# A DLRM tower with three interaction layers on one core: two steps of 32 rows in front, the top network in five chunks, and layer 1's sums on ScalarE

## Chip, core and metric

The kernel runs on one core of a Trainium2 chip. The metric is device time in microseconds (us), here the median of three executions. Five engines matter: TensorE (PE; its weight loads are shown as PEld), VectorE (DVE), ScalarE (ACT), GpSimd (POOL), and SyncE (SP), whose queue issues nearly all transfers. Each engine takes its own instructions in order; semaphores order the engines among themselves.

## What is computed

For 1024 batch rows, 32 table rows of 16 numbers are looked up (one of each table), which gives `e` with shape (1024, 32, 16). Three layers of pairwise products follow, each summed over the last dimension; the 192 sums and 16 dense numbers go through a small network.

```python
x0 = xk = e                                    # (1024, 32, 16)
for W in (W0, W1, W2):                         # (32, 32, 64), (32, 64, 64), (32, 64, 64)
    xk = relu(einsum('bmd,bhd,mhk->bkd', x0, xk, W))
    outs.append(sum(xk, axis=2))
z = concatenate(outs, axis=1)                  # (1024, 192)
h = concatenate([z, dense_ctx], axis=1)        # (1024, 208)
h = maximum(h @ W_top1 + b_top1, 0)            # 512
h = maximum(h @ W_top2 + b_top2, 0)            # 256
y = h @ W_top3                                 # (1024, 1)
```

All numbers are float32.

## The kernel before

**Steps.** The batch is cut into 16 steps of 64 rows. With 16 numbers a row, a step has 1024 columns (`PAIR`), handled as two halves of 512. Both halves of a layer's result lie in one PSUM bank: half 0 in partitions 0 to 63, half 1 in 64 to 127.

**Tiles.** For layers 1 and 2 the 32 x 64 = 2048 pairs (m, h) make 16 tiles of 128 partitions. A tile of x0, shifted by so many fields, is multiplied element by element with x1 or x2, and PE contracts the product with that tile's 64-column weights into the bank, one matmul for each half (`contract`). The trace shows each float32 matmul as two records, so a tile is four records. Layer 0 uses symmetry: one matmul pair over the squares and four tiles.

**Who multiplies.** DVE makes the products of layer 0 (two groups of two tiles) and of most tiles of layers 1 and 2, two tiles in one instruction (`product`), into a ring of four groups (`RING`, `prod`). POOL makes the last 3 tiles of layers 1 and 2 (5 and 4 in the last two steps, `POOL_LAST`), into a ring of four tiles. `POOL_BEFORE` says ahead of which DVE group PE takes each of POOL's tiles.

**Data in.** POOL gathers the rows of step s+2 with 16 indirect DMAs, spread between its tiles of step s: after the three tiles of layer 1 come 1, 1 and 8 gathers, after those of layer 2 come 1, 1 and 4. For the first two steps it issues all 32 gathers at the start. SP stores the gathered rows of a step to a scratch tensor in memory (`store_rows`), waits for that, loads the step's `x0g` (one transfer) and its 16 shifted tiles `x0bc` (`load_tiles`). `x0bc` has 24 slots of one tile, so tile j of step s waits until the product of 24 tiles earlier is made. SP does all this in program order.

**ACT.** For each layer, `finish` reads the bank: four ACTIVATEs spread relu(result) into x1_ps or x2_ps for DVE (`spread_done`), one writes `relu` in SBUF, four copy that to x1_sb or x2_sb for POOL (`copied`). Layer 2 has none of those; its 32 sums a step are made by 32 ACTIVATEs of 16 columns with an accumulator output, each followed by a read of the accumulator (L373). The sums of layers 0 and 1 are made by DVE, one TENSOR_REDUCE each (`sums`, L314). ACT also copies x0g into PSUM for DVE's layer 0 (`place_x0g`, L353) and squares it (L358).

**Order.** DVE runs layer 1 of step s, layer 0 of step s+1, sums of layer 0, layer 2 of step s, sums of layer 1. PE uses the same order over two banks that alternate (`STAGES`, `y_bank`), and waits for ACT to be done with a bank. ACT's order within a step:

```python
for s in range(STEPS):
    if s < LAST:
        place_x0g(s + 1)
        square(s + 1)
    finish(s, 1, x2_ps, x2_sb)
    if s < LAST:
        finish(s + 1, 0, x1_ps, x1_sb)
    else:
        mlp(range(MLP_EARLY))
    finish(s, 2)
mlp(range(MLP_EARLY, len(MLP)))
```

**Top network.** It works on two chunks of 512 rows. Its weights are loaded into free `x0bc` slots near the end. The first layer of chunk 0 (`MLP_EARLY`, 16 matmul records on PE) runs between layers 1 and 2 of the last step; everything else comes behind the last layer 2, and the 1024 results leave in one transfer.

Of the kernel before, what the change touches and what calls it, by code (L numbers as in the profile page):

```python
# [6 lines left out]
I32 = mybir.dt.int32  # L7
# [18 lines left out]
STEPS = COLS // PAIR  # L26
STEP_B = BATCH // STEPS
HALF_B = STEP_B // 2
QUART = P // FIELDS
GATHERS = STEP_B // QUART  # L30
# [15 lines left out]
POOL_LAST = {STEPS - 2: (5, 4), STEPS - 1: (5, 4)}  # L46
POOL_COUNT = [POOL_LAST.get(s, (3, 3)) for s in range(STEPS)]
POOL_BEFORE = {3: [2, 3, 5], 4: [2, 3, 4, 5], 5: [2, 3, 4, 5, 5]}
GATHERS_AFTER = {1: [1, 1, 8], 2: [1, 1, 4]}

# [29 lines left out]
def pool_after(x):  # L80
# [3 lines left out]
MLP = ([(1, 0, j) for j in range(HID1 // P)] + [(2, 0, j) for j in range(HID2 // P)] +  # L84
       [(1, 1, j) for j in range(HID1 // P)] + [(3, 0, 0)] + [(2, 1, j) for j in range(HID2 // P)] + [(3, 1, 0)])
MLP_EARLY = HID1 // P
MLP_BANKS = 4
LAST = STEPS - 1

# [5 lines left out]
def cin_tower_kernel(nc, table, ids, id_offset, dense_t, w0_a, w0_b, w0_sq, w1, w2,  # L95
                     wt1_a, wt1_b, bt1, wt2, bt2, wt3, x0_rows, out):
    with ExitStack() as ctx:
# [9 lines left out]
        ids_sb = sb("ids_sb", [P, STEPS * GATHERS], I32)  # L107
        off_sb = sb("off_sb", [P, STEPS * GATHERS], I32)
        row_sb = sb("row_sb", [P, STEPS * GATHERS], I32)
# [13 lines left out]
        z = sb("z", [P, 3, STEPS * HALF_B])  # L123
# [25 lines left out]
        mlp_ps = [x0g_ps[:, 0, :], x0g_ps[:, 1, :], x1_ps[:, 0, :], x1_ps[:, 1, :]]  # L149
# [387 lines left out]
```

## Time and profile before

| what | before |
|---|---|
| median of 3 runs | 637.69 us (637.17 to 637.77) |
| the profiled execution's own time | 638.89 us |
| span of its trace | 637.1 us |
| PE busy | 563.1 us (88%) |
| DVE busy | 548.7 us (86%) |
| POOL busy | 488.3 us (77%) |
| ACT busy | 302.5 us (47%) |
| transfers on SP's queue | 148.4 MB, 63.6% of 16 engines |

Busy shares are averages over stages with different limits: a front of about 60 us, a steady part, and a tail of about 50 us behind the last layer 1. Matmul records overlap, so a busy PE isn't PE at its peak. In what follows, (s, l) is layer l of step s, and "layer 0 of step s+1" is run by all engines behind (s, 1).

### The profile page before, as it was taken

How to read it: one execution, taken by the hardware profiler on the slowest of the kernel's cores; microseconds unless marked ns; L12 is line 12 of the kernel's file. 1: busy time of each engine (PE TensorE's matmuls, PEld its weight loads, DVE VectorE, ACT ScalarE, POOL GpSimd, SP SyncE). 2: the span in 40 equal slices, each digit the busy share in tenths (PEclk: the TensorE clock that was granted, in tenths of full speed). 3: DMA queues.
4: the chain of work that ended last, by engine and by line, in shares of the span. 5: the costliest groups of instructions: out<-in, count | busy, mean ns of one | idle time of the engine just before them, and what ended most of it. 6: DMA issues, size and time to landing. Idle time of an engine off the chain costs nothing.

```text
span 637.1 us, 7625 instructions
## 1 busy us (share of the span) xinstructions
PE 563.1 (88%) x2440; PEld 178.9 (28%) x2440; DVE 548.7 (86%) x330; ACT 302.5 (47%) x1359; POOL 488.3 (77%) x364
## 2 busy tenths in 40 slices
PE   0058998999999998999899999999999989999998
PEld 0012232332323232332223232323232322333332
DVE  0038998999999999999999999999999999897810
ACT  0023637354545646364535456464736454544352
POOL 6756898869888888979898788888897989584500
PEclk9997999999999999999999999999999999999999
DMA  3298857677876867686778768686868587871000
GB/s 105 39 391 312 307 200 284 240 298 263 306 274 227 295 217 270 244 299 214 297 274 306 268 238 315 211 298 215 307 213 319 225 302 266 307 284 49 1 1 0
DMA packets 52843, 151.01 MB, mean 237 GB/s; under 512 B 9697, under 2 KB 17377, under 8 KB 52802
## 3 DMA queue, kind: packets, MB, share of 16 engines
q1 hardware_dynamic: 44610, 148.40, 63.6%
q0 software_dynamic: 8192, 2.11, 2.5%
q8 instruction: 19, 0.31, 0.2%
q14 instruction: 22, 0.18, 0.1%
HBM read 147.33 MB, written 3.15 MB: 236 GB/s over the span
## 4 chain that ended last, share of the span: by engine, by line
DVE 36%; PE 24%; DMA 19%; issue 10%; POOL 8%; SPq 2%; ACT 1%; DVEq 0%; POOLq 0%
DVE prod L286 34%; PE y_ps L417 20%; DMA x0bc<-x_rows 15%; POOL emb L247 6%; DVE z L314 2%; DMA emb<-table,row_sb 2%; DMA x_rows<-emb 2%; POOL pool_prod L260 1%; SPq L214 1%; PE x_ps L477 1%; ACT relu L373 1%; PE x0g_ps L477 1%; PE x_ps L470 1%; PE x0g_ps L470 1%; PE x0g_ps L471 1%
## 5 line engine op out<-in xcount | busy, mean ns | idle before, releaser
L286 DVE TENSOR_TENSOR prod<-x0bc,x_ps 128x2048 f32<-128x2048 f32 (+1 forms) x252 | 456.0, 1878 | 8.6 <-ACT x_ps L368 8.6
L417 PE MATMUL y_ps<-prod,w_sb 128*64 128x512 f32 x1640 | 384.9, 599 | 27.8 <-DVE prod L286 27.8
L247 POOL DMA_INDIRECT emb<-table,row_sb x256 | 244.9, 957 | 65.5 <-issue 63.7
L260 POOL TENSOR_TENSOR pool_prod<-x0bc,x_sb 128x1024 f32<-128x1024 f32 x102 | 242.3, 2382 | 45.7 <-ACT x_sb L383 36.3
L417 PEld LDWEIGHTS y_ps<-prod,w_sb 128*64 128x64 f32 x1640 | 115.5, 137 | 280.1 <-issue 219.7
L373 ACT ACTIVATE relu<-y_ps 128x16 f32<-128x16 f32 x512 | 84.5, 287 | 144.3 <-PE y_ps L417 144.3
L368 ACT ACTIVATE x_ps<-y_ps 64x512 f32<-64x512 f32 x128 | 73.0, 570 | 78.5 <-PE y_ps L417 75.8
L417 PE MATMUL y_ps<-pool_prod,w_sb 128*64 128x512 f32 x408 | 105.0, 595 | 1.5 <-POOL pool_prod L260 1.3
L286 DVE TENSOR_TENSOR prod<-x0bc,x0g_ps 128x2048 f32<-128x2048 f32 x32 | 72.6, 2282 | 38.5 <-DMA x0bc<-x_rows 35.3
L373 ACT ACTIVATION_READ_ACCUMULATOR relu<-y_ps 128x1 f32 x512 | 84.7, 315 | 0.2
L383 ACT ACTIVATE x_sb<-relu 64x512 f32<-64x512 f32 x128 | 80.4, 628 | 3.4
L417 PE MATMUL y_ps<-prod,w0s_sb 128*64 128x512 f32 x256 | 61.6, 617 | 5.4 <-DVE prod L286 5.4
L353 ACT ACTIVATE x0g_ps<-x0g 128x1024 f32<-128x1024 f32 x16 | 16.4, 1028 | 90.1 <-DMA x0g<-x_rows 90.1
L417 PE MATMUL y_ps<-squares,wsq_sb 128*64 128x512 f32 x64 | 17.4, 623 | 35.6 <-ACT squares L358 35.6
L417 PEld LDWEIGHTS y_ps<-pool_prod,w_sb 128*64 128x64 f32 x408 | 28.3, 137 | 62.7 <-issue 47.8
L417 PEld LDWEIGHTS y_ps<-prod,w0s_sb 128*64 128x64 f32 x256 | 18.1, 141 | 47.1 <-issue 29.3
L314 DVE TENSOR_REDUCE z<-relu 128x32 f32<-128x512 f32 x32 | 21.6, 676 | 0.0
L378 ACT ACTIVATE relu<-y_ps 128x512 f32<-128x512 f32 x32 | 19.1, 597 | 0.8
L417 PEld LDWEIGHTS y_ps<-squares,wsq_sb 128*64 128x64 f32 x64 | 4.6, 141 | 44.1 <-issue 44.1
L358 ACT ACTIVATE squares<-x0g 128x1024 f32<-128x1024 f32 x16 | 16.7, 1041 | 0.0
L327 DVE COPY x0bc<-z 64x256 f32<-64x256 f32 x12 | 3.4, 286 | 11.6 <-ACT relu L373 11.3
L477 PE MATMUL x0g_ps<-x0bc 128*128 128x512 f32 x24 | 10.7, 597 | 0.0
(29 smaller groups left out, 49.2 us busy)
## 6 DMA issues: line engine op xcount, KB each, us to landing
x0bc<-x_rows SPq DMA_DIRECT2D x256, 512.0 KB, 6.8
x0g<-x_rows SPq DMA_DIRECT2D x16, 512.0 KB, 4.7
emb<-table,row_sb POOLq DMA_INDIRECT x256
x_rows<-emb SPq DMA_DIRECT2D x16, 128.0 KB, 2.1
w_sb<-w SPq DMA_DIRECT2D x2, 512.0 KB, 4.6
x_rows<-emb SPq DMA_DIRECT2D x16, 64.0 KB, 2.0
x0bc<-wt SPq DMA_DIRECT2D x1, 512.0 KB, 5.4
x0bc<-wt_a SPq DMA_DIRECT2D x1, 256.0 KB, 4.1
```

What stands on the lines that cost most here:

```text
L247: pool.indirect_dma_start(emb[:, turn, DIM * n:DIM * (n + 1)], None, table, bass.IndirectOffsetOnAxis(row_sb[:, at:at + 1], 0)).then_inc(g ...
L260: pool.tensor_tensor(pool_prod[:, n % POOL_RING, :], x0bc[:, slot(s, j), :], x[:], ALU.mult).then_inc(pool_products, 1)
L286: made = dve.tensor_tensor(prod[:, n % RING, 0:count, cols], tiles[:, :, cols], right.unsqueeze(1).to_broadcast([P, count, right.shape[1]] ...
L314: dve.tensor_reduce(z[:, l, s * HALF_B:(s + 1) * HALF_B], relu[:, l, :].rearrange("p (b d) -> p b d", d=DIM), AX_X, ALU.add).then_inc(summ ...
L353: act.activation(x0g_ps[:].rearrange("p h c -> p (h c)"), x0g[:], ACT.Copy).then_inc(x0g_placed, 1)
L358: act.activation(squares[:], x0g[:], ACT.Square).then_inc(squared, 1)
L368: act.activation(x[MAPS * copy:MAPS * (copy + 1), h, :], ps[MAPS * h:MAPS * (h + 1), :], ACT.Relu).then_inc(spread_done[l], 1)
L373: act.activation(relu[:, l, DIM * b:DIM * (b + 1)], ps[:, DIM * b:DIM * (b + 1)], ACT.Relu, accum_out=z[:, l, s * HALF_B + b:s * HALF_B + ...
L378: act.activation(relu[:, l, :], ps[:], ACT.Relu).then_inc(relu_done[l], 1)
L383: act.activation(x_sb[MAPS * copy:MAPS * (copy + 1), HALF * h:HALF * (h + 1)], relu[MAPS * h:MAPS * (h + 1), l, :], ACT.Copy).then_inc(cop ...
L417: made = pe.matmul(ps[MAPS * h:MAPS * (h + 1), :], w, moving[:, HALF * h:HALF * (h + 1)], start=first, stop=final)
L477: made = pe.matmul(ps[0:rows, :], w[:, k, :], x[:, k, :], start=k == 0, stop=k == ks - 1)
```

## The change

Four things are done at once.

1. The steps become 17: two of 32 rows, then 15 of 64. All widths become functions of the step. POOL has no tiles in step 0 and three half-wide tiles a layer in step 1. At the start POOL issues 8 + 8 + 16 gathers, for three steps. `off_sb` is one column, broadcast.
2. The top network runs in five chunks (steps 0 to 4, 5 to 8, 9 to 12, 13 to 15, and 16; 256, 256, 256, 192 and 64 rows). A chunk that ends ahead of step s (`TURN`: s = 5, 9, 13, 16) has its first layer on PE behind layer 0 of step s+1, its second behind (s, 2), and its third inside (s+1, 1) ahead of group 1. For s = 16 the second and third stand inside (16, 2), ahead of groups 2 and 4. They use x0g_ps as their bank. ACT makes the transposed input (`mlp_input`, 6 small copies, 12 for chunk 0), all relus, the copy of y, and issues the output transfer of each chunk. All weights have buffers of their own and are loaded by SP behind the tiles of step 1.
3. The sums of layer 1 move from DVE to ACT: 32 accumulating copies a step (`sums1`), read from `relu` in SBUF.
4. The sums of layer 2 in the last step alone go to DVE as one TENSOR_REDUCE; the last chunk's first layer adds its layer-2 part last (`last_chunk`).

The core of the diff:

```diff
-STEPS = COLS // PAIR
+ROWS_OF = [32, 32] + [64] * 15
+STEPS = len(ROWS_OF)
...
-POOL_LAST = {STEPS - 2: (5, 4), STEPS - 1: (5, 4)}
+POOL_OF = {0: (0, 0), STEPS - 2: (5, 4), STEPS - 1: (5, 4)}
...
+CHUNKS = [(0, 5), (5, 9), (9, 13), (13, 16), (16, 17)]
+FINAL = len(CHUNKS) - 1
+TURN = {end: c for c, (_, end) in enumerate(CHUNKS[:FINAL])}
...
 # SP
                 load_x0g(s)
                 load_tiles(s)
+                if s == 1:
+                    for dst, src in ((wt1a_sb[:], wt1_a), (wt1b_sb[:], wt1_b), (wt2_sb[:], wt2), (wt3_sb[:], wt3),
+                                     (bt1_sb[:], bt1), (bt2_sb[:], bt2), (zt_b[MAPS:, :], dense_t)):
+                        sp.dma_start(dst, src).then_inc(mlp_in, 16)
...
 # POOL
-            gather(0, 0, GATHERS)
+            gather(0, 0, GATHERS_OF[0])
             pool.wait_ge(rows_done, 2)
-            gather(1, 0, GATHERS)
+            gather(1, 0, GATHERS_OF[1])
+            gather(2, 0, GATHERS_OF[2])
...
 # DVE
                 sums(s, 0)
-                if s == LAST:
-                    mlp_input(0)
                 layer(s, 2, x2_ps)
-                sums(s, 1)
-            mlp_input(1)
+            sums(LAST, 2)
+            last_input()
...
 # ACT
+            def sums1(s):
+
+                for b in range(ROWS_OF[s] // 2):
+                    cols, at = slice(DIM * b, DIM * (b + 1)), FIRST_ROW[s] // 2 + b
+                    act.activation(spare[:, cols], relu[:, 1, cols], ACT.Copy,
+                                   accum_out=z[:, 1, at:at + 1]).then_inc(act_summed1, 1)
...
             for s in range(STEPS):
+                if s - 1 in TURN:
+                    hidden2(TURN[s - 1])
+                    output(TURN[s - 1])
+                if s in TURN:
+                    mlp_input(TURN[s], range(3))
                 if s < LAST:
                     place_x0g(s + 1)
                     square(s + 1)
                 finish(s, 1, x2_ps, x2_sb)
                 if s < LAST:
                     finish(s + 1, 0, x1_ps, x1_sb)
-                else:
-                    mlp(range(MLP_EARLY))
+                sums1(s)
+                if s in TURN:
+                    hidden1(TURN[s])
+                if s == LAST:
+                    hidden2(TURN[s])
+                    output(TURN[s])
+                    mlp_input(FINAL, range(2))
                 finish(s, 2)
-            mlp(range(MLP_EARLY, len(MLP)))
+            hidden1(FINAL)
+            hidden2(FINAL)
+            output(FINAL)
...
 # PE
+            def hidden2(c):
+                n = CHUNK_ROWS[c]
+                pe.wait_ge(mlp_act, PIECES_OF_CHUNK * c + H1_TILES)
+                for j in range(H2_TILES):
+                    for k in range(H1_TILES):
+                        made = pe.matmul(x0g_ps[:, 0, CHUNK_B * j:][:, 0:n], wt2_sb[:, k, P * j:P * (j + 1)],
+                                         h1[:, k, 0:n], start=k == 0, stop=k == H1_TILES - 1)
+                made.then_inc(mlp_mm, 1)
+
+            def output(c):
+                n = CHUNK_ROWS[c]
+                pe.wait_ge(mlp_act, PIECES_OF_CHUNK * c + H1_TILES + H2_TILES)
...
             for s in range(STEPS):
-                layer(s, 1, w1_sb)
+                layer(s, 1, w1_sb, {1: lambda: output(TURN[s - 1])} if s - 1 in TURN else {})
                 if s < LAST:
                     layer0(s + 1)
+                if s in TURN:
+                    pe.wait_ge(mlp_in, 16 * 7)
+                    hidden1(TURN[s])
+                if s == LAST:
+                    layer(s, 2, w2_sb, {2: lambda: hidden2(TURN[s]), 4: lambda: output(TURN[s])})
                 else:
-                    pe.wait_ge(mlp_in, 16 * 7)
-                    mlp(range(MLP_EARLY))
-                layer(s, 2, w2_sb)
-            mlp(range(MLP_EARLY, len(MLP)))
+                    layer(s, 2, w2_sb)
+                    if s in TURN:
+                        hidden2(TURN[s])
+            last_chunk()
```

## Rows read from the trace of the kernel before

**Rows 1.** Stages: length, busy of PE, PEld, DVE, ACT, POOL, clock, DMA share, GB/s.

```profile
36.50:61.00 24.50, 18.83 (x60) 5.02 (x58) 19.01 (x10) 6.34 (x10) 14.16 (x12) 0.86 0.93 342
102.00:554.00 452.00, 425.15 (x1918) 133.68 (x1916) 445.24 (x259) 235.86 (x1090) 382.95 (x282) 1.00 0.74 266
608.50:637.10 28.60, 24.95 (x58) 9.36 (x56) 1.73 (x6) 11.93 (x74) 0.00 (x0) 1.00 0.00 0
```

**Rows 2.** Waits from 102 to 554 us: total, times, longest.

```profile
ACT relu L373 <- PE y_ps L417: 114.7, 13, 9.8
...
ACT x0g_ps L353 <- DMA x0g<-x_rows: 45.6, 13, 4.3
...
POOL pool_prod L260 <- ACT x_sb L383: 14.2, 13, 2.6
...
DVE prod L286 <- DMA x0bc<-x_rows: 5.5, 7, 1.9
```

**Rows 3.** Groups by line and form: busy us, mean ns | idle before them.

```profile
L373 ACT ACTIVATION_READ_ACCUMULATOR relu<-y_ps 128x1 f32 x512 | 84.7, 315 | 0.2
L373 ACT ACTIVATE relu<-y_ps 128x16 f32<-128x16 f32 x512 | 84.5, 287 | 144.3 <-PE y_ps L417 144.3
L383 ACT ACTIVATE x_sb<-relu 64x512 f32<-64x512 f32 x128 | 80.4, 628 | 3.4
...
L378 ACT ACTIVATE relu<-y_ps 128x512 f32<-128x512 f32 x32 | 19.1, 597 | 0.8
...
L353 ACT ACTIVATE x0g_ps<-x0g 128x1024 f32<-128x1024 f32 x16 | 16.4, 1028 | 90.1 <-DMA x0g<-x_rows 90.1
```

**Rows 4.** The chain that ended last, 343 to 385 us: start, us, what.

```profile
344.28 1.89 DVE prod L286
...
348.76 0.60 DVE z L314
...
365.85 2.34 DMA emb<-table,row_sb
...
372.09 6.01 DMA x0bc<-x_rows
...
378.63 2.11 DVE prod L286
```

**Rows 5.** POOL's timeline in the same stretch: start, us, instruction.

```profile
352.45 2.37 POOL L260 TENSOR_TENSOR pool_prod<-x0bc,x_sb 128x1024 f32<-128x1024 f32 x1 [2.06 <-ACT x_sb L383]
...
366.80 2.38 POOL L260 TENSOR_TENSOR pool_prod<-x0bc,x_sb 128x1024 f32<-128x1024 f32 x1
```

**Rows 6.** Timeline of all engines, 0 to 60 us.

```profile
13.37 0.94 POOL L247 DMA_INDIRECT emb<-table,row_sb  x1 [0.30 <-issue]
...
23.35 0.94 POOL L247 DMA_INDIRECT emb<-table,row_sb  x1 [0.30 <-issue]
...
29.33 10.80 SPq L214 DMA_DIRECT2D x0bc<-x_rows  x16
...
36.46 4.71 DVE L286 TENSOR_TENSOR prod<-x0bc,x0g_ps 128x2048 f32<-128x2048 f32 x2 [27.12 <-DMA x0bc<-x_rows]
...
45.04 2.35 ACT L368 ACTIVATE x_ps<-y_ps 64x512 f32<-64x512 f32 x4 [9.57 <-PE y_ps L417]
```

**Rows 7.** Timelines of POOL and DVE, 60 to 110 us.

```profile
86.40 2.38 POOL L260 TENSOR_TENSOR pool_prod<-x0bc,x_sb 128x1024 f32<-128x1024 f32 x1
...
101.99 2.29 DVE L286 TENSOR_TENSOR prod<-x0bc,x0g_ps 128x2048 f32<-128x2048 f32 x1 [1.88 <-DMA x0bc<-x_rows]
```

**Rows 8.** The chain over the whole span, its tail.

```profile
587.56 1.06 PE x0g_ps L470 x2
...
594.64 13.91 PE y_ps L417 x64
608.57 5.38 ACT relu L373 x64
616.10 1.10 PE x_ps L470 x2
```

More of the change, by code:

```diff
@@ L25 @@
 PAIR = 2 * HALF
-STEPS = COLS // PAIR
-STEP_B = BATCH // STEPS
-HALF_B = STEP_B // 2
+ROWS_OF = [32, 32] + [64] * 15
+STEPS = len(ROWS_OF)
+FIRST_ROW = [sum(ROWS_OF[:s]) for s in range(STEPS + 1)]
 QUART = P // FIELDS
-GATHERS = STEP_B // QUART
+GATHERS_OF = [n // QUART for n in ROWS_OF]
+GATHERS = max(GATHERS_OF)
 TILES = FIELDS * MAPS // P
@@ L251, in layer @@
             def layer(s, l, x):
+                if not pool_tiles(s, l):
+                    return
                 gathers = GATHERS_AFTER[l]
@@ L279, in _, with product @@
         def _(dve):
-            def product(n, count, tiles, x, h=None):
+            def product(s, n, group, x, h=None):
                 if n >= RING and h != 1:
                     dve.wait_ge(products_used, n - RING + 1)
-                cols = slice(0, PAIR) if h is None else slice(HALF * h, HALF * (h + 1))
-                right = x[:].rearrange("p h c -> p (h c)")[:, cols]
-                made = dve.tensor_tensor(prod[:, n % RING, 0:count, cols], tiles[:, :, cols],
-                                         right.unsqueeze(1).to_broadcast([P, count, right.shape[1]]), ALU.mult)
+                at, count = slot(s, group[0]), len(group)
+                halves = slice(0, 2) if h is None else slice(h, h + 1)
+                out, left = (t.rearrange("p t (h c) -> p t h c", h=2)[:, :, halves, :]
+                             for t in (prod[:, n % RING, 0:count, 0:width(s)], x0bc[:, at:at + count, 0:width(s)]))
+                right = x[:, halves, 0:half(s)].unsqueeze(1).to_broadcast(list(left.shape))
+                made = dve.tensor_tensor(out, left, right, ALU.mult)
                 if h != 0:
@@ L294, in layer0 @@
                     dve.wait_ge(bc_in[g], 32 * (s + 1))
-                    at = slot(s, group[0])
-                    product(before((s, 0)) + g, GROUP, x0bc[:, at:at + GROUP, :], x0g_ps)
+                    product(s, before((s, 0)) + g, group, x0g_ps)
             def layer(s, l, x):
@@ L301, in layer @@
                         dve.wait_ge(bc_in[g], 32 * (s + 1))
-                    n, at, count = before((s, l)) + g, slot(s, group[0]), len(group)
-                    tiles = x0bc[:, at:at + count, :]
+                    n = before((s, l)) + g
                     if g == 0:
@@ new lines, in output @@
+            def output(c):
+                n, first = CHUNK_ROWS[c], FIRST_ROW[CHUNKS[c][0]]
+                act.wait_ge(mlp_mm, BANKS_OF_CHUNK * c + (H1_TILES + H2_TILES + 1 if c == FINAL else 4))
+                if c > 0:
+                    act.wait_ge(stored, 16 * c)
+                ps = final_ps[2] if c == FINAL else x0g_ps[:, 1, :]
+                act.activation(y_sb[:, 0:n], ps[0:1, 0:n], ACT.Copy).then_inc(mlp_act, 1)
+                act.wait_ge(mlp_act, PIECES_OF_CHUNK * (c + 1))
+                act.dma_start(out[first:first + n, :].rearrange("b o -> o b"),
+                              y_sb[:, 0:n]).then_inc(stored, 16)
@@ new lines, in hidden1 @@
+            def hidden1(c):
+                n, first = CHUNK_ROWS[c], FIRST_ROW[CHUNKS[c][0]]
+                b = slice(first, first + n)
+                pe.wait_ge(zt_ready, inputs_after(c))
+                for j in range(H1_TILES):
+                    ps, out_f = x0g_ps[:, j // 2, CHUNK_B * (j % 2):][:, 0:n], slice(P * j, P * (j + 1))
+                    pe.matmul(ps, wt1a_sb[:, out_f], zt_a[:, 0:n], start=True, stop=False)
+                    made = pe.matmul(ps, wt1b_sb[:, out_f], zt_b[:, b], start=False, stop=True)
+                    if j % 2 == 1:
+                        made.then_inc(mlp_mm, 1)
```

265 lines of the change are left out of this document (155 added, 110 removed).

## The prediction

> **What bounds the kernel now.** I read the stages first. From 102 to 554 us, 13 steps, DVE is busy 445 of 452 us, PE 425, POOL 383 and ACT 236 [rows 1]: 34.8 us a step, with DVE as the engine that hardly rests. The reader is to see there that three engines are nearly full and ACT is half empty. Behind 608.5 us DVE does almost nothing and PE still has 25 us of work in 28.6: that tail is the top network and nothing else.
>
> The waits of the same stretch say what else ends late. DVE stands 5.5 us in seven waits for x0bc [rows 2]. The chain shows the loop behind it [rows 4, 5]: (s, 1) ends on DVE at 344.28, POOL starts its layer 2 at 352.45 once ACT has copied x, is done at 366.80, the last gather lands at 368.2, SP stores, loads x0g, then x0bc, which lands at 378.10; DVE needs it at 378.63. So from the end of (s, 1) to the data of layer 0 one step later there are 33.8 us (call it L), while DVE takes 378.63 - 344.28 = 34.35 us for a step. L is a near tie here, and where transfers land later it is above and DVE waits. POOL's own step is just as long: layer 2 takes 366.80 - 352.45 = 14.35 us, layer 1 has four more gathers at (23.35 - 13.37) / 8 = 1.25 us [rows 6], so 19.35, together 33.7.
>
> **Part 1, two steps of 32 rows.** The eighth gather starts at 13.37 and the sixteenth at 23.35 [rows 6]: step 0 is stored 10.0 us earlier. x0bc transfers are issued 5.98 us behind the sixteenth gather's start, hence at 19.35. They landed 36.46 - 29.33 = 7.1 us later with 1.57 MB (x0g and a group) to move; at 342 / 0.93 = 368 GB/s [rows 1] that is 4.3 us, and half the bytes save 2.1 of it: 5.0. DVE starts at 24.4, not 36.5. PE runs at 1.2 GHz here (granted clock 0.86 on average from 36.5 to 61 [rows 1], so half speed for part of it), so ACT gets its result about 4.7 us later, at 29.2 (before 45.04 [rows 6]). Layer 1 of 32 rows is 16 tiles at half of 2.28 / 2, some 9.5 us, as POOL has none: 39.5. Gathers of step 1 have long landed, but SP issues 16 transfers in 10.8 us, to 30.2, and the store then queues behind them: x0bc of step 1 at about 35.6, landed at 40. (0, 2) starts when a slow PE lets it, about 43.5, and ends at 53. Tiles 8 to 15 of step 1 wait for slots that (0, 2) frees, until 49; the seven weight loads stand behind them on SP at up to 0.6 us each, and the store, x0g and x0bc of step 2 behind those: issued about 56.4, landed 63.5 for the first group and 66.1 for the second. Layer (1, 1) ends on DVE at 60.8, so DVE stalls there, and (1, 2) ends about 76.6.
>
> POOL can start (1, 1) at about 51, when tiles 12 and 13 are in, and has 15.8 us there (three half tiles save 3.6) and 10.8 in (1, 2): done at 77.6, against 86.40 before. x0bc's second group landed 15.6 us behind that point (101.99 [rows 7]), so 93.2; DVE itself arrives at 93.3. Gain 8.8 us at that point, after which both kernels have 13 steps and the tail. Bounds: 5 if the slow clock or the weights cost more, 11 if neither is felt.
>
> **Part 3, layer 1's sums.** It takes one TENSOR_REDUCE a step from DVE, 0.60 us [rows 4]: DVE's step becomes 33.75. A step of DVE's time is not the whole, since L goes from the end of one (s, 1) to the layer 0 after the next: where L binds, two steps take DVE's time plus L. With L between 33.8 (the quiet stretch) and 35.2 (34.8 a step before is the mean of 34.35 and 35.2) the step becomes 33.8 to 34.5, and POOL's 33.7 forbids less. Gain 0.3 to 1.0 a step, at most 0.6 of it from the reduce alone; I take 0.42, 5.5 us over 13 steps, bounds 3.5 and 7.8.
>
> On ACT the price is that of L373, the same form but read from PSUM. Each pair shows 287 + 315 ns, yet all 512 are busy 84.5 and 84.7 us [rows 3], since they overlap: 32 pairs took 5.38 us in the chain [rows 8]. Reading SBUF, L383's 64x512 took 628 ns where L378's 128x512 from PSUM took 597, so add up to 0.03 to 0.06 each: 5.4 to 7 us. Where does it lie? ACT idles 114.7 / 13 = 8.8 us ahead of layer 2's sums [rows 2]. It fits: nothing on the path, and if that cover were gone each us over 8.8 would delay ACT's in-order queue, first the release of the bank and place_x0g, on which DVE's next layer 0 waits.
>
> The Trainium skill, "ScalarE: Activation LUTs", section "Rules for kernel authors", speaks against this: a relu, add or multiply belongs on VectorE, and an ACTIVATE is to be budgeted at about 0.3 us plus 0.83 ns an element. By that, as an estimate, 32 copies would take 10 us and not fit into 8.8; the row's 0.17 us a copy is the measurement, and I go by it.
>
> **Part 2, the network in chunks.** mlp_input is 6 small copies (12 for chunk 0); ACT waits 45.6 / 13 = 3.5 us for x0g at that place [rows 2]: free. hidden1's four relus of up to 256 columns are about 0.4 us each (597 ns for 512, 1028 for 1024 [rows 3], so 0.43 less for each 512 less): 1.6 us into the 8.8 - 5.4 that are left. On PE hidden1 and hidden2 are 16 records of 256 columns each, half of 0.214, 1.7 us apiece. hidden1 mostly fits where PE waits for DVE's first group.
>
> output does not fit. A tile on PE takes 13.91 / 16 = 0.87 us [rows 8], so a layer of 16 tiles takes as long as DVE's 14.4, and a delay inside it lasts to its end. Let DVE end (s, 2) at E. PE is done at E+2.5 (DVE's last group must be contracted, estimate from the 16 tiles), hidden2 until 4.2. ACT makes 32 sums until E+7.9, then two relus until 8.8. PE stands in (s+1, 1) ahead of group 1 until these are done, at about E+9.2, where it would have gone on at E+4.7. Queued behind it are 14 tiles. DVE, four groups ahead, is stopped by the ring in layer 0 for 1.6 us, and by x2_ps for another 1.4: (s+1, 2) starts 3.0 us late. x for POOL comes 4.5 us late, thus POOL's gathers and x0bc two steps on, a further 1 to 2 us, of which stalls that exist anyway absorb part. I take 3.5 for each of the three turns (s = 5, 9, 13): +10.5, bounds 3 and 18. ACT's output transfer and y copy precede place_x0g and stay inside its 3.5 us.
>
> **The tail.** PE ends the last layer 1 at 587.56; call that X. Before, the end is X+49.5. Now: ACT spreads (2.35 [rows 6]), relu and copies to X+5.6, sums1 to 11.0, hidden1's relus to 12.3. PE waits ahead of group 2 for those, does hidden2 (about 1.6 us) and then 12 tiles at 0.87 and output: X+24.7. The last chunk of 64 rows: relu 0.6, reduce 0.7, two copies 0.4, 8 + 16 + 4 short records about 3.2, relus and y about 2, transfer about 2: 8.9. End X+33.7, gain 15.8. It consists of 7 us of early matmuls and 28.6 of network and sums against a 4.6 us stall and 8.9. Bounds 13 and 18; the short records are priced from none of this trace's, between their share of 0.214 us and the whole of it.
>
> **Sum.** -8.8 - 5.5 + 10.5 - 15.8 = -19.6 us. Against the profiled execution's own 638.89 (span 637.1 and 1.8 around it) that gives 619.3; that execution is 1.2 above the median, so 618.1: 618.
>
> **Rivals.**
> *Turns hidden, 0.20.* The stalls at output fall into waits for x0bc that exist anyway, each costs 1 us, and the reduce is won in full: 637.7 - 8.8 - 7.8 + 3 - 15.8 = 608. For it: seven waits for x0bc in 13 steps. Against: they sum to 5.5 us.
> *Turns dear, 0.17.* With POOL at 33.7 of 33.8 us a step, 4.5 us of lateness isn't made up until the next turn; PE then waits for POOL's tiles too. Each turn costs 6, the reduce gives 3.5: 637.7 - 8.8 - 3.5 + 18 - 15.8 = 628.
> *Front lost, 0.07.* Weight loads and slow clock hold step 2, so the gain at its x0bc is nil: 618 + 8.8 = 627.
> *Slower, 0.04.* The copies from SBUF don't overlap with their accumulator reads and take the 0.60 us that the records show: 19.3 us a step. ACT then has 236 / 13 + 19.3 = 37.4 us for a step of 34.4, 3.0 more over 14 steps, and 618 + 42 = 660. It costs from 8.8 / 32 = 0.27 us a copy on, and decides the sign where 14 steps give back 19.7 us: a step of 35.8 us, 0.55 us a copy. Against it: 5.38 us for 32. Here too belongs the skill's 0.3 us rule above; by it the copies pass the 8.8 us by about 1.2, which costs time but not the sign.
>
> **Numbers.** The forecast has 0.52 and its own range of 612 to 624. The range 605 to 629 takes in the cheap and dear turns and the lost front, at their bounds, and leaves out the slower case and the ends. A change under 0.2% couldn't be told from none by three runs that lie within 0.1%. Faster 0.95, within that 0.01, slower 0.04.
>
> **What the profile after would show.** First x0bc product near 24.4 us. POOL's (1, 2) done near 77.6. sums1 in 5.4 to 7 us with an idle stretch of 2 us or more left ahead of layer 2's sums. DVE's interval 33.75 where nothing waits, 33.8 to 34.5 on average away from turns. Ahead of each output a PE wait of about 4.5 us for ACT, and (s+1, 2) about 3 us late. The last PE tile 24 to 25 us behind the last layer 1, the end 9 us later. I am wrong if ACT's sums aren't hidden, if POOL's lateness adds up, or if x0bc lands later because loads crowd.

## The result: slower by 3.1%, and the profile after

| what | before | after |
|---|---|---|
| median, timed side by side | 637.73 us (637.17 to 638.97, 4 runs) | 656.52 us (654.81 to 663.71, 4 runs) |
| ratio of the means | 1 | 1.0313, interval 1.0235 to 1.0392 |
| profiled execution, own time | 638.89 us | 655.63 us |
| span of its trace | 637.1 us | 653.8 us |

The forecast was 618 us. I cut both spans at two points that every kernel of this study has. F is the start of DVE's second layer 0 product of the step that begins at row 128, T the same in the last step.

| stretch | before | after | change | predicted |
|---|---|---|---|---|
| start to F | 101.99 | 113.40 | +11.4 | -8.8 |
| F to T, 13 steps | 452.1 | 469.2 | +17.1 | +5.0 (turns +10.5, sums -5.5) |
| T to end | 83.0 | 71.2 | -11.8 | -15.8 |
| span | 637.1 | 653.8 | +16.7 | -19.6 |

Three stages of after, to be held against [rows 1]: length, busy of PE, PEld, DVE, ACT, POOL, granted clock, DMA share, GB/s.

```profile
26.50:61.00 34.50, 17.86 (x124) 9.49 (x124) 18.69 (x19) 10.12 (x26) 13.34 (x15) 0.80 0.55 170
113.40:582.60 469.20, 450.65 (x2034) 152.05 (x2032) 439.57 (x246) 334.91 (x1970) 384.26 (x283) 1.00 0.71 256
615.90:653.80 37.90, 27.89 (x138) 15.98 (x136) 14.43 (x10) 17.45 (x92) 9.34 (x4) 0.86 0.00 1
```

In the middle one PE is busy 25.5 us more than before (450.65 against 425.15) and DVE 5.7 us less: PE has become the engine that hardly rests. The waits say so too. These are waits of after from F to T (total, times, longest), against [rows 2]:

```profile
ACT x_ps L407 <- PE y_ps L514: 58.4, 12, 9.5
...
ACT x0g_ps L391 <- DMA x0g<-x_rows: 25.2, 10, 4.6
...
DVE prod L330 <- PE y_ps L514: 14.3, 10, 1.9
```

DVE waits for PE, in ten pieces, 14.3 us in all; its waits for x0bc, 5.5 us before, are down to 1.3. The front of after, against [rows 6]:

```profile
21.58 0.60 ACT L391 ACTIVATE x0g_ps<-x0g 128x512 f32<-128x512 f32 x1 [19.56 <-DMA x0g<-x_rows]
...
26.52 2.53 DVE L330 TENSOR_TENSOR prod<-x0bc,x0g_ps 128x1024 f32<-128x1024 f32 x2 [16.97 <-issue]
27.80 3.68 PE L514 MATMUL y_ps<-prod,w0s_sb 128*64 128x256 f32 x16 [3.80 <-issue]
...
37.72 25.19 SPq L256 DMA_DIRECT2D x0bc<-x_rows  x16
43.91 1.50 ACT L407 ACTIVATE x_ps<-y_ps 64x256 f32<-64x256 f32 x4 [21.17 <-remote]
```

PE is done with the first bank at 31.48 (27.80 + 3.68), yet ACT copies it from 43.91 on, after a wait of 21.17 us that the profile puts down to no engine's work ("remote"). I call this the late start; 12.4 us pass there with DVE and PE idle.

One turn of after (chunk 0, PE unless marked):

```profile
222.72 0.70 PE L565 MATMUL x0g_ps<-zt_a,wt1a_sb 128*128 128x256 f32 x2
...
225.86 0.59 PE L566 MATMUL x0g_ps<-zt_b,wt1b_sb 80*128 80x256 f32 x2
226.39 3.65 PE L514 MATMUL y_ps<-prod,w_sb 128*64 128x512 f32 x16
...
240.27 3.72 PE L575 MATMUL x0g_ps<-h,wt_sb 128*128 128x256 f32 x16
243.92 1.94 PE L514 MATMUL y_ps<-prod,w_sb 128*64 128x512 f32 x8
245.40 1.09 ACT L469 ACTIVATE h<-x0g_ps,bt_sb 128x256 f32<-128x256 f32 x2
...
246.54 1.02 PE L583 MATMUL x0g_ps<-h,wt_sb 128*1 128x256 f32 x4 [0.68 <-ACT h L469]
247.49 1.94 PE L514 MATMUL y_ps<-prod,w_sb 128*64 128x512 f32 x8
```

The first layer takes 226.39 - 222.72 = 3.67 us, the second 243.92 - 240.27 = 3.65, the third 0.95 behind a wait of 0.68. A turn so takes 8.95 us out of PE's time, 8.27 of them work. The tail of after:

```profile
615.89 0.59 PE L565 MATMUL x0g_ps<-zt_a,wt1a_sb 128*128 128x192 f32 x2
...
621.87 1.94 PE L514 MATMUL y_ps<-prod,w_sb 128*64 128x512 f32 x8 [0.17 <-DVE prod L330]
629.37 4.48 PE L575 MATMUL x0g_ps<-h,wt_sb 128*128 128x192 f32 x16 [5.56 <-ACT h L462]
```

PE stands 5.56 us for ACT's relus, which are queued behind the 32 sums, and the 16 matmuls behind that wait take 4.48 us.

### The profile page after: what moved, and what is told of

It reads as the page before. It is cut to its first block, busy times and chain, and to the rows that moved or that the text cites. A ratio compares the mean times of both kernels' runs of the same rounds, so it can differ in the third digit from the quotient of the medians.

```text
span 653.8 us, 9203 instructions
## 1 busy us (share of the span) xinstructions
PE 572.0 (87%) x2696; PEld 205.6 (31%) x2696; DVE 543.4 (83%) x326; ACT 415.0 (63%) x2395; POOL 481.6 (74%) x364
## 4 chain that ended last, share of the span: by engine, by line
PE 40%; DVE 19%; DMA 15%; issue 12%; ACT 6%; POOL 6%; SPq 3%; DVEq 0%
PE y_ps L514 36%; DVE prod L330 18%; DMA x0bc<-x_rows 10%; POOL emb L284 3%; ACT relu L414 2%; POOL pool_prod L299 2%; DMA emb<-table,row_sb 2%; DMA x_rows<-emb 2%; DVE z L358 1%; DMA x0g<-x_rows 1%; SPq L256 1%; ACT spare L434 1%; PE x0g_ps L565 1%; PE x0g_ps L566 1%; PE x0g_ps L575 1%
## 5 line engine op out<-in xcount | busy, mean ns | idle before, releaser
L330 DVE TENSOR_TENSOR prod<-x0bc,x_ps 128x2048 f32<-128x2048 f32 (+2 forms) x270 | 460.4, 1776 | 32.1 <-issue 17.8
L514 PE MATMUL y_ps<-prod,w_sb 128*64 128x512 f32 (+1 forms) x1768 | 386.4, 569 | 30.6 <-issue 21.5
L299 POOL TENSOR_TENSOR pool_prod<-x0bc,x_sb 128x1024 f32<-128x1024 f32 (+1 forms) x102 | 235.8, 2317 | 80.8 <-ACT x_sb L426 47.0
L407 ACT ACTIVATE x_ps<-y_ps 64x512 f32<-64x512 f32 (+1 forms) x136 | 74.1, 545 | 119.8 <-PE y_ps L514 71.6
L330 DVE TENSOR_TENSOR prod<-x0bc,x0g_ps 128x2048 f32<-128x2048 f32 (+1 forms) x34 | 73.2, 2160 | 47.1 <-issue 35.9
L514 PE MATMUL y_ps<-pool_prod,w_sb 128*64 128x512 f32 (+1 forms) x408 | 102.9, 584 | 4.9 <-POOL pool_prod L299 4.7
L434 ACT ACTIVATE spare<-relu 128x16 f32<-128x16 f32 x512 | 101.9, 200 | 0.8 <-issue 0.4
L434 ACT ACTIVATION_READ_ACCUMULATOR spare<-relu 128x1 f32 x512 | 95.9, 187 | 2.0 <-issue 2.0
L426 ACT ACTIVATE x_sb<-relu 64x512 f32<-64x512 f32 (+1 forms) x136 | 82.1, 603 | 3.6
L514 PE MATMUL y_ps<-prod,w0s_sb 128*64 128x512 f32 (+1 forms) x272 | 63.4, 601 | 7.6 <-issue 6.7
L575 PE MATMUL x0g_ps<-h,wt_sb 128*128 128x256 f32 (+1 forms) x64 | 15.6, 404 | 5.6 <-ACT h L462 5.6
```

Source lines behind the costliest of these rows:

```text
L299: pool.tensor_tensor(pool_prod[:, n % POOL_RING, 0:width(s)], x0bc[:, slot(s, j), 0:width(s)], x[:, 0:width(s)], ALU.mult).then_inc(pool_p ...
L330: made = dve.tensor_tensor(out, left, right, ALU.mult)
L407: act.activation(x[MAPS * copy:MAPS * (copy + 1), h, 0:half(s)], ps[MAPS * h:MAPS * (h + 1), 0:half(s)], ACT.Relu).then_inc(spread_done[l], 1)
L426: act.activation(x_sb[MAPS * copy:MAPS * (copy + 1), half(s) * h:half(s) * (h + 1)], relu[MAPS * h:MAPS * (h + 1), l, 0:half(s)], ACT.Copy ...
L434: act.activation(spare[:, cols], relu[:, 1, cols], ACT.Copy, accum_out=z[:, 1, at:at + 1]).then_inc(act_summed1, 1)
L514: made = pe.matmul(ps[MAPS * h:MAPS * (h + 1), 0:half(s)], w, moving[:, half(s) * h:half(s) * (h + 1)], start=first, stop=final)
```

## The experiments

All kernels are variants of before or of after. The table has the points of each profiled execution and "first copy", the start of ACT's first copy out of a layer 0 bank (L368 before, L407 to L410 in the variants). A ratio is to the kernel before, timed beside it on the same chip; "-" is a single execution. F, T and the first copy come from one execution each, so small differences between them mean little: F to T is 467.5, 469.2 and 472.1 us in the three profiles of after (r5, after, r14), and 470.1 to 475.9 in the four of e1.

| run | first copy | F | F to T | T to end | ratio (interval) |
|---|---|---|---|---|---|
| before | 45.04 | 101.99 | 452.1 | 83.0 | 1 |
| after | 43.91 | 113.40 | 469.2 | 71.2 | 1.0313 |
| e1 sums on DVE | 30.50 | 105.09 | 470.1 | 63.5 | 1.0067 (1.0037 to 1.0098) |
| e2 before, sums on ACT | 45.36 | 101.74 | 448.8 | 83.0 | 0.9989 (0.9973 to 1.0005) |
| e3 even steps | 45.75 | 104.48 | 473.5 | 71.2 | 1.0193 (1.0163 to 1.0224) |
| e4 no turns | 31.55 | 105.38 | 450.6 | 71.3 | 0.9848 (0.9804 to 0.9891) |
| r5 after again | 50.69 | 120.44 | 467.5 | 71.3 | 1.0333 (1.0285 to 1.0381) |
| e6 weights late | 50.88 | 119.83 | 470.5 | 71.3 | 1.0348 (1.0286 to 1.0411) |
| e7 last sums behind | 50.84 | 121.24 | 468.9 | 63.6 | 1.0256 (1.0190 to 1.0321) |
| e10 spread | 47.88 | 117.75 | 452.7 | 67.7 | 1.0029 (0.9995 to 1.0063) |
| e11 even, spread | 49.62 | 105.62 | 456.7 | 67.9 | 0.9772 (0.9719 to 0.9824) |
| r12 before again | 49.70 | 104.58 | 451.1 | 83.0 | - (640.47 us) |
| r13 e1 again | 51.23 | 120.65 | 475.9 | 64.3 | - (662.75 us) |
| r14 after again | 51.81 | 121.79 | 472.1 | 71.5 | - (667.23 us) |
| e15 gather behind | 30.08 | 105.20 | 472.5 | 65.2 | 1.0080 (1.0054 to 1.0105) |
| r16 e1 again | 30.26 | 104.80 | 470.9 | 65.2 | 1.0088 (1.0061 to 1.0115) |
| e17 spread, gather behind | 31.61 | 105.87 | 452.6 | 66.2 | 0.9825 (0.9799 to 0.9852) |
| e18, r19 (e15 and e1 again) | 30.66, 30.58 | 103.32, 105.18 | 473.5, 471.5 | 64.7, 63.8 | - |
| e20 after, gather behind | 30.89 | 116.72 | 473.3 | 71.6 | 1.0253 (1.0217 to 1.0290) |

### The parts of the change, one by one

**e1_dve_sums** puts layer 1's sums back on DVE:

```diff
                 layer(s, 2, x2_ps)
+                sums(s, 1)
...
-                sums1(s)
```

> The changed kernel with layer 1's sums back on DVE, one TENSOR_REDUCE a step. Theory A (the sums on ACT are hidden and give DVE 0.6 us a step back, the losses lie elsewhere): 3 to 8 us slower than the changed kernel's 656.5, about 661. Theory B (the 512 extra accumulating copies on ACT delay something, for instance signals from PE that ACT waits for): faster than 656.5, and the 12 us idle stretch of ACT between 31.5 and 43.9 us and the waits of 1 to 1.6 us ahead of layer 0's results vanish. If that first stretch stays, it isn't these copies, which come later.

Measured: 642.20 us, and the idle stretch is gone, as theory B had it. Theory B is wrong all the same: the same kernel met the stretch later (r13), so it isn't made by these copies.

**e2_act_sums** is the kernel before with those sums alone moved to ACT:

```diff
                 layer(s, 2, x2_ps)
-                sums(s, 1)
...
-                else:
+                sums1(s)
+                if s == LAST:
                     mlp(range(MLP_EARLY))
```

> The kernel before with this one part alone: layer 1's sums by 32 accumulating copies a step on ACT. Theory A: 3.5 to 7.8 us faster than before, 630 to 634, as DVE's step becomes 33.75 us. Theory B: no gain or a loss, 637 or more, with ACT standing idle for PE's results that PE had long finished.

Measured in e2: 637.07 us, the ratio's interval includes 1, and ACT doesn't stand idle for results that are long there. In the one profile F to T is 3.3 us shorter. DVE's step is shorter by the reduce, and the time hardly is. In after the 32 copies of one step run from 231.4 to 238.2 on ACT, 0.21 us each, the size that was forecast. In e1 the last stretch is 7.7 us shorter than in after (63.5 against 71.2), and PE's wait ahead of the network's second layer is gone. So ACT's sums are free in the steady part and cost about 7.7 us in the tail of after (at least 6.0, as the other profiles with turns and DVE's sums have 63.8 to 65.2). In e2 they cost nothing in the tail either, 83.0 us as before: there PE needs none of ACT's relus until the last layer 2 is done.

**e3_even_steps** is after with 16 steps of 64 rows and no third gather at the start.

```diff
-ROWS_OF = [32, 32] + [64] * 15
+ROWS_OF = [64] * 16
...
-CHUNKS = [(0, 5), (5, 9), (9, 13), (13, 16), (16, 17)]
+CHUNKS = [(0, 4), (4, 8), (8, 12), (12, 15), (15, 16)]
...
-            gather(2, 0, GATHERS_OF[2])
```

> The changed kernel with 16 steps of 64 rows (chunks of 4, 4, 4, 3 and 1 steps) and two steps' gathers in front, as before. Theory A (the short steps cost 11.4 us, since layer 0's second group of the step that begins at row 128 came at 113.4 us and before at 102.0): 656.5 - 11.4, about 645, and that group at 102 us or a little later. Theory B (the front's stall doesn't come from the short steps): it stays above 650 with an idle stretch of ACT in the front.

F is at 104.48, as good as in e1 and e4 with the 32-row steps (105.09, 105.38): the two short steps bring nothing even where ACT starts on time. Theory A has the front right, though the time, 650.57 us, is not its 645: F to T is 473.5 us, 24.7 longer than in e2 and 4.3 longer than in after. Single profiles of one kernel lie up to 5.8 us apart there, so this may be no more than spread; no run settles it.

**e4_no_turns** leaves out the top network of rows 0 to 767 (chunks 0 to 2), so those outputs are not computed; all else is as in after.

```diff
-TURN = {end: c for c, (_, end) in enumerate(CHUNKS[:FINAL])}
+CHUNKS = [(13, 16), (16, 17)]
+FINAL = 1
+TURN = {16: 0}
```

> The changed kernel with the top network left out for its first three chunks (rows 0 to 831 get no output); the chunk of steps 13 to 15 and the last one stay. Theory A (PE is the bound around a turn: hidden1 and hidden2 took 3.5 and 3.7 us there where 1.7 each were forecast, output 1.6 with its wait, so each turn costs 6 to 7 us): 656.5 - 20, about 636. Theory B (the turns cost the 3.5 us each that were forecast and the rest of the loss is contention): about 646.

F to T is 450.6 us against 469.2 in after: the three turns cost 18.65 us, 6.2 each (16.9 to 21.6 by r5 and r14). Theory A has the turns right. The time of 629.01 us is 7 us below its 636, as F is 8.0 us sooner than in after.

**r5_same_again** and **e6_weights_late** ask what the weight loads cost; e6 issues them behind the tiles of step 3.

```diff
-                if s == 1:
+                if s == 3:
```

> The changed kernel, nothing altered. In its first profile ACT began layer 0's results of step 0 at 43.9 us, though PE's last record for them ended at 31.5, and the versions without ACT's sums or without the network's first chunks don't show that wait. Theory A (it belongs to that execution, not to the code): the first product of layer 1 comes near 32.5 us here, layer 0 of the third step ends near 77 us rather than 86, and the time is 645 to 648 from the other parts' sum. Theory B (it belongs to this code): the wait is there again and the time is 654 to 660.

> The changed kernel with the seven loads of the top network's weights behind the tiles of step 3, not of step 1. Theory A (these loads, 5 us of SP's queue and 1 MB ahead of the third step's store, delay that step's data): its store starts some 5 us earlier and lands 2 to 3 us sooner, and the kernel is 4 to 7 us faster than the changed one. Theory B (POOL or the slots of x0bc hold the front anyway): within 1 us of it.

The two times are alike (662.35 and 662.89 us), and F differs by 0.6 us. The loads aren't free, though: without them DVE starts layer 0 of the step that begins at row 64 at 82.22 us, with them at 87.46. F doesn't follow. Both show where ACT starts on time as well. This is the chain of e1, with the loads (L271) on it from 54.08 until the store (L229) at 58.38; at its end x0bc for F leaves when a product of DVE has freed its slot, at 96.43:

```profile
54.08 0.59 SPq L271
...
58.38 0.57 SPq L229
58.99 5.03 DMA x_rows<-emb
64.04 4.78 DMA x0g<-x_rows
...
94.22 2.21 DVE prod L330
96.43 0.11 SPq L256
...
97.24 7.83 DMA x0bc<-x_rows
```

With the loads behind the next step (e17) that layer 0 starts at 69.68 instead of e1's 71.95, and F is at 105.87 instead of 105.09. No run has the loads out of the front altogether with ACT on time.

**e7_sums_behind** moves the last step's sums behind the relus of the network's second layer on ACT.

```diff
-                sums1(s)
+                if s < LAST:
+                    sums1(s)
...
                     hidden2(TURN[s])
+                    sums1(s)
                     output(TURN[s])
```

> The changed kernel with ACT's 32 sums of layer 1 in the last step moved behind the two layers of chunk 3's network, so that PE, which stands ahead of group 2 of the last layer for ACT's relus, gets them 6.6 us sooner. Theory A (ACT's order makes the tail's stall of 5.6 us): 5 to 6.5 us faster than the changed kernel. Theory B (the tail is held by PE's matmuls alone): no more than 1 us.

PE in its tail, the place that answers to 629.37 of after:

```profile
629.45 1.94 PE L516 MATMUL y_ps<-prod,w_sb 128*64 128x512 f32 x8 [0.17 <-DVE prod L330]
631.32 2.87 PE L577 MATMUL x0g_ps<-h,wt_sb 128*128 128x192 f32 x16
```

No wait, and the same 16 records take 2.87 us instead of 4.48. The stall of 5.56 us had cost 1.6 us more behind it: from 629 to 634 us the granted clock is 0.63 in after, so for most of that time the lower of its two levels (1.2 and 2.4 GHz), and 1.00 in e7. Measured: T to end 63.6 against 71.3, and 656.77 us against 662.35 for r5, as theory A had it.

### Spreading the network

**e10_spread** has the chunks (0, 4), (4, 8), (8, 12), (12, 16), (16, 17), the sums on DVE and the weight loads behind step 2, and cuts each of the first three networks into four pieces: half of the first layer, the other half, half of the second, the rest with the output, one piece a step.

```diff
+PIECE = {CHUNKS[c][1] + i: (c, i) for c in range(3) for i in range(4)}
...
 # PE, behind layer 0 of step s+1
                 if s in TURN:
                     pe.wait_ge(mlp_in, 16 * 7)
+                if s in PIECE:
+                    c, i = PIECE[s]
+                    if i < 2:
+                        hidden1(c, range(2 * i, 2 * i + 2))
+                    else:
+                        hidden2(c, range(i - 2, i - 1))
+                if s == LAST:
                     hidden1(TURN[s])
```

> Layer 1's sums on DVE as before the change, weights loaded behind step 2, and each of the first three chunks' network cut into four pieces of 8 matmul records of at most 256 columns (1.7 us of PE each by the 0.217 us a record that the turns showed), one a step, behind layer 0; the third layer goes inside layer 2 ahead of group 4. Theory A (a step leaves PE 2 to 3 us, so small pieces fit and 8.8 us at once don't): the turns' 18 us shrink to 5 to 9 and the weights give 4: 627 to 633. Theory B (PE has no room at all, each record costs its length wherever it stands): the sum of the matmuls stays, 636 to 640.

Two of chunk 0's pieces, a half of the first layer and a half of the second, and the stretch F to T as in [rows 1]:

```profile
191.28 0.59 PE L573 MATMUL x0g_ps<-zt_a,wt1a_sb 128*128 128x192 f32 x2
...
192.37 0.49 PE L574 MATMUL x0g_ps<-zt_b,wt1b_sb 80*128 80x192 f32 x2
...
260.98 1.57 PE L583 MATMUL x0g_ps<-h,wt_sb 128*128 128x192 f32 x8
```

```profile
117.75:570.49 452.74, 442.80 (x2022) 150.18 (x2020) 445.45 (x260) 247.32 (x1131) 381.79 (x279) 1.00 0.75 267
```

PE carries the work of the turns as well (442.80 us busy, 17.65 more than before) in 452.7 us, the length of before's 13 steps. A step of before left PE (452.0 - 425.15) / 13 = 2.07 us [rows 1]. A piece of 1.6 to 2.0 us goes into that; a turn's 8.95 us in two steps does not, and 8.95 less the room of the two steps it touches, 4.1, leaves 4.8 of the 6.2 us measured. That sum is an estimate; that spreading helps is measured. The same work costs 18.65 us in three turns and 0.6 in twelve pieces. The time of 644.03 us is above both theories all the same, for this run met the late start (F at 117.75). The pair without it, on one chip, is e15 with turns and e17 with pieces, both below: 643.42 and 627.34 us, F to T 472.5 and 452.6.

**e11_even_spread** is e10 with even steps, chunks (0, 3), (3, 7), (7, 11), (11, 15), (15, 16) and no third gather at the start.

> The spread network (four pieces of a chunk, one a step, layer 1's sums on VectorE) with 16 even steps of 64 rows and without the third gather at the start, chunks of 3, 4, 4, 4 and 1 steps. If the 32-row steps are what made the front long, and the pieces cost nothing: the front point is that of the kernel before, 102 to 104.5 us, the steady part is its 452, and the end follows the last layer 0 by the spread kernel's 67.7 us: a span of 622 to 625, own time 624 to 627, ratio 0.978 to 0.983 to the kernel before. If the 32-row front cost nothing but a chance wait, the time is that of the spread kernel, ratio 1.00. If the four pieces in even steps meet a full PE, each of the 12 pieces costs 1 to 2 us: ratio 1.00 to 1.02.

It took 629.38 us against 643.36 beside it: 2.3% faster than before. Its gain is the tail (67.9 against 83.0 us). F to T is 456.7 us, 4.6 to 5.6 more than in the two profiles of before (452.1 and 451.1), so in this one execution the pieces weren't free; why is open.

### The late start

In the table the first copy with a 32-row front is at 30 to 32 us or at 44 to 52. Three more runs on e11's chip:

> The kernel before, unchanged, for a profile on the chip of this job. If ScalarE's late start in front (its first bank of layer 0 is copied 12 to 20 us after PE's last matmul for it) belongs to a chip or an execution, this run can show such late signals too, if this chip has them: bank copies later than PE's record by more than 1 us, and a front point later than 102. If it belongs to the 32-row front alone, none is seen here: front point 101.5 to 102.5, steady 452.

> The changed kernel with layer 1's sums on VectorE, unchanged from its first run, which had no late start in front (front point 105). If the late start is of the chip or execution, it appears here whenever it appears in the other kernels of this job with the 32-row front; if it is made by ScalarE's sums, it does not: front point 105, against 113 to 120 for the changed kernel beside it.

> The changed kernel, unchanged. If the late start in front is of the chip or execution, it appears here together with the same kernel with VectorE's sums, or in neither; if it is made by the code of the change, here alone: front point 113 to 121, ScalarE's first bank copy at 44 to 51 us.

The first copy of the kernel before, of e1 in the first group, and of the same e1 here, one line of three timelines:

```profile
49.70 2.35 ACT L368 ACTIVATE x_ps<-y_ps 64x512 f32<-64x512 f32 x4 [14.18 <-remote]
```

```profile
30.50 1.50 ACT L408 ACTIVATE x_ps<-y_ps 64x256 f32<-64x256 f32 x4 [7.37 <-PE y_ps L514]
```

```profile
51.23 1.50 ACT L408 ACTIVATE x_ps<-y_ps 64x256 f32<-64x256 f32 x4 [28.21 <-remote]
```

So it isn't made by the change: the same kernel shows it in one run and not in another, and the kernel before has it too. It also isn't a fixed delay: on this chip the copy starts at 49.6 to 51.8 us whether the bank is ready at 30 or at 45. Before's bank is ready at 45.0 anyway, so its copy starts 4.7 us late and F comes 2.6 later; with a 32-row front, ready at 30, the copy starts 20.7 us late and F of e1 goes from 105.09 to 120.65. The earlier the change makes this bank, the more of its gain can be taken back here.

Two more things go with it. A wait that ends by "remote" stands in all ten profiles with a late start, 4 to 9 of them on ACT (in after 32.9 us in nine: the 21.17 and eight of at most 1.7 us from F to T), and in none of the other ten. And SP is slower in seven of the ten: its first 16 x0bc transfers take 13.9 to 15.6 us to issue in e6, e7, r5, r13 and r14, against 12.0 to 12.5 in the others with 32 rows, and 17.4 in r12 and e11 against 10.8 to 11.3 with 64. So more than PE's signal to ACT is held. Not everything is: in e20 below ACT takes up x0g at 40.20 with the gathers under way.

What is under way in that time in every kernel are POOL's 32 gathers, whose last starts at 43.21 in r13. **e15_gather_behind** stops them half-way; **r16** is its control, **e17** does the same to e10.

```diff
+            pool.wait_ge(copied[0], 4)
             gather(2, 0, GATHERS_OF[2])
```

> The changed kernel with layer 1's sums on VectorE, and the third gather (16 indirect DMAs of step 2, at the start) held until ScalarE has made step 0's first copies. If GpSimd's gathers delay PE's signal to ScalarE: with the hold they pause at 24 us, ScalarE's first bank copy begins right behind PE, at 30 to 32 us, on any chip, and where the control r16 shows it at 44 to 52 us this kernel is 10 to 15 us faster than the control. If the gathers are not it: the first copy begins as late as in the control, and the time is the control's or 0 to 3 us more, as step 2's gathers start later.

> The control: the changed kernel with layer 1's sums on VectorE, as in its two runs before. On a chip with the late start: first bank copy at 48 to 52 us and ratio 1.02 to 1.03; on one without: at 30 to 32 us and ratio 1.007.

> The spread kernel (ratio 1.003 with the late start) with the same hold of the third gather. If the gathers make the late start, the 32-row front comes 10 to 15 us earlier than in the spread kernel's first run: front point near 105, span 105 + 452.7 + 67.7 = 625, ratio 0.975 to 0.985. If not: as before the hold, ratio 1.00 to 1.01 on a chip with the late start, 0.98 on one without.

No kernel of that group showed the late start, so it tells nothing of the gathers; it does tell that the hold is free (643.42 us with and without) and that the spread network with a 32-row front on time is worth 1.8%, no more than with even steps. The pair was run once more, again without a late start:

> As e15: if GpSimd's gathers delay PE's signal, the first bank copy begins at 30 to 32 us here though the control beside it shows 44 to 52. If they do not, it begins as late as in the control. If the control shows 30 to 32, this chip has no late start and the pair tells nothing.

> The control of e18: first bank copy at 44 to 52 us on a chip with the late start, at 30 to 32 us on one without.

**e20_after_behind** is after itself with the hold.

> The changed kernel, all as in the change, with the third gather held until ScalarE's first copies. On a chip without the late start (first bank copy at 30 to 32 us): front point 105, steady part 467 to 469, last part 71.3, so a span of 644 to 646 and an own time of 646 to 648, ratio 1.013 to 1.018; that is the change without the late start. On a chip with it (if the kernel before beside it takes 641 or more): first copy at 30 to 32 and ratio 1.01 if the gathers delay the signal, first copy at 44 to 52 and ratio 1.03 if they do not.

It met the late start, on the chip on which e1 and e4 had had none; before took 643.24 us beside it, and 637.89 beside those. The expectation for that case had 1.01 if the gathers are the cause and 1.03 if not; measured are 1.0253, with the first copy on time and F at 116.72 all the same. Its front:

```profile
30.89 1.50 ACT L408 ACTIVATE x_ps<-y_ps 64x256 f32<-64x256 f32 x4 [7.90 <-PE y_ps L515]
...
34.83 0.94 POOL L284 DMA_INDIRECT emb<-table,row_sb  x1 [10.74 <-ACT x_sb L427]
...
45.86 1.22 DVE L331 TENSOR_TENSOR prod<-x0bc,x0g_ps 128x1024 f32<-128x1024 f32 x1 [4.83 <-remote]
...
53.55 0.94 POOL L284 DMA_INDIRECT emb<-table,row_sb  x1 [0.30 <-issue]
...
57.80 1.50 ACT L408 ACTIVATE x_ps<-y_ps 64x256 f32<-64x256 f32 x4 [16.34 <-remote]
```

With the gathers held, the first copy comes right behind PE, at 30.89. Then the gathers run from 34.83 to 54.5, DVE and ACT have "remote" waits of 4.8, 6.5 and 16.3 us, and the copy of the next bank, that of (0, 1), is at 57.80, 3.3 us behind the last gather (in e15 it was at 41.40). The waits moved with the gathers. That speaks for the gathers as one of two conditions, the other being something that differs from one time to another on one chip. But it is one profile, without a control beside it, and the end of the gathers alone doesn't set the end of the wait: in r13 the copy came 7 us behind the last gather, in after 0.2 us ahead of its end. The cause stays open.

## Why the prediction was wrong

**What failed.** Of the error of 36.3 us in the span (+16.7 instead of -19.6), 20.2 lie in the front, 12.1 in the turns and sums, 4.0 in the tail.

1. *Front, "5 if the slow clock or the weights cost more, 11 if neither is felt".* Wrong in sign. The first product came at 26.5 for my 24.4, so the early steps held. Then two things failed. First, 8.0 us of late start (113.40 against e4's 105.38), which no row of before showed. Second, the chain from POOL's (1, 2) on: without a late start F is at 103.3 to 105.9, not 93.2. Even steps have it at 104.48, so shortening the first two steps gives nothing; why even that is 2.5 us behind before's 101.99, no run shows. In e1 x0bc of step 1 is issued until 54.0 for my "until 49", as its transfers wait for slots; POOL starts (1, 1) at 57.49 for my 51 (before: 52.43), and step 2's x0bc goes out at 64.6 for my 56.4, with 4.3 us of weight loads ahead of it. I had left SP's issue of 16 transfers at 10.8 us [rows 6]; 16 half-wide ones took 12.13. I priced the lead of 10 us at the start and carried it through a chain that is paced by slots and by SP. The rival "front lost" (0.07, no gain) came nearest, and of the causes that it names the weight loads are on the chain, the slots are not among them.

2. *Turns, "16 records of 256 columns each, half of 0.214, 1.7 us apiece".* This is the term that was mis-sized most: 3.65 us a layer. The 0.214 is what a record with 64-column weights adds, 13.91 / 64 of a layer [rows 8]; one with 128-column weights adds about twice that. The row that had the price was in [rows 8] as well: 16 such records, of 512 columns, from 587.56 to 594.64, 0.44 us each. By it a turn holds 3.5 + 3.5 + 1 = 8 us of PE, 3.9 more than the 4.1 us of room in two steps; measured are 6.2. The number of the rival "turns dear" (6 each) came out by luck: its mechanism, POOL's lateness that adds up, is not what the runs show. Nor is mine: I let PE's work fit and made the wait for ACT the cause, 4.5 us ahead of each output. It measured 0.68 in the first turn, since PE's own work hid it, and it is PE's full time that makes the turns dear (e10, and e17 against e15).

3. *Layer 1's sums, -5.5.* F to T without turns is 450.6 (e4) and 448.8 (e2) for 452.1: 1.5 to 3.3 us, below my lower bound of 3.5, and e2's time shows no gain clear of noise. The step that failed is how much of DVE's 0.6 us a step reaches the whole. That L binds more than I let it would explain it; no run shows that.

4. *ACT's price of the sums.* Right: 32 copies in 5.4 to 7 us, forecast from L373's overlap. The "slower" rival's mechanism (0.60 us a copy, on the path) did not happen; that its 660 us lies nearest to the 656.5 measured is chance. Measured are 0.21 us a copy of 16 columns. The Trainium skill, "ScalarE: Activation LUTs", section "Rules for kernel authors", budgets about 0.3 us plus 0.83 ns an element for an ACTIVATE with a bias operand, by which 16 columns take an estimated 0.31. `sums1` passes no bias, so I had carried the rule to a case that it isn't stated for, and the trace's 0.21 is below it.

5. *Tail, -15.8, measured -11.8.* X is at 615.9 and the end at X + 37.9 for my X + 33.7. The second layer took 4.48 us for my 1.6 (the same mis-sizing, 2.87, and 1.6 of slow clock, 0.63 granted), and the stall 5.6 for my 4.6. The last 8.7 us (653.8 - 645.1) are my 8.9. The bounds 13 and 18 were missed. The 15.8 comes from the timetable; the parts that I listed behind it (7 and 28.6 against 4.6 and 8.9) sum to 22.1, since they leave out PE's work on the network inside the last layer 2.

**What held:** PE's wait ahead of group 2, its place and cause (e1, e7), the end behind the last tile, the sums' cover in the steady part.

The sign was wrong even without the late start: after would then have stood at 1.014 to 1.019. That is an estimate: front +3.4, turns and sums +17.1 and tail -11.8 sum to +8.7 us, or e1's ratio of 1.0067 to 1.0088 plus the 7.7 us of the sums in the tail less the 0.9 that they give from F to T.

## What to carry to other kernels

When work is put between the matmuls of a full loop, first divide that engine's idle time by the steps, price the new records by rows with the same weight width, and cut the work into pieces that fit; here the turns' 18.65 us became 0.6 (452.7 against 452.1; 4.6 in e11), and without ACT's sums 3.1% slower became 1.8% faster with the 32-row steps on time (e17) and 2.3% faster with even ones (e11), each against the kernel before beside it. Of a lead at the start count only what the slowest link behind it (slots, one queue) lets through, and try the plain version beside it. In-order work that is free in the loop can be dear in the last step, where it should stand last.

## What the runs showed of the hardware that I had not expected

- The late start: ACT took up a bank 12 us and more behind PE's record for it, in after, e6, e7, e10, r5, r13, r14 and e20 (there the second bank), 4.5 to 4.8 us behind in r12 and e11, and at once in e1 to e4 and e15 to r19 (where the bank is ready at 45, as in e2 and e3, a hold that ends before that can't be seen); the same kernel took 642.20 and 662.75 us with and without it. Where before ran beside such kernels its median was 642.0 to 643.4 us, elsewhere 637.9 to 638.3, with one exception: 637.73 beside after itself, whose first copy was at 43.91. In seven of these ten profiles SP issued its first 16 x0bc transfers more slowly too (13.9 to 17.4 us for 10.8 to 12.5). What makes it is open.
- A matmul record with 128-column weights and 256 columns took 0.23 us (3.65 / 16), one with 192 columns 0.18 (2.87 / 16), one with 512 columns 0.44 ([rows 8]). One with 64-column weights and 512 columns, of two that write different halves of a bank, took 0.22 (0.87 a tile of four, [rows 8]), as if two ran side by side; no run separates the two.
- A PE stall of 5.56 us cost 1.6 us more in the 16 records behind it (4.48 against 2.87), at a granted clock of 0.63 against 1.00 from 629 to 634 us (after, e7).
- Sixteen transfers of half the width took SP longer to issue (12.13 us in e1) than sixteen full ones (10.80 in before, 11.34 in e3).
